# Two-layer mixed network on one core: the wave stage written out over two buffers, and five layers' loads issued ahead of their norms

## The chip, the core and the metric

The kernel runs on one core of a Trainium2 chip. A core has TensorE (matrix products), VectorE, ScalarE, GpSimd and a queue engine, SyncE, that issues transfers. They run side by side and meet at semaphores. The metric is the device time of one execution in microseconds (us).

## What is computed

`x` is 4 x 512 x 256 in float32. Six layers follow each other, each of the form x = x + f(norm(x)): a gated delta net, masked cross attention over 1601 context rows, a ternary MLP, a selective scan followed by a wave term, full cross attention over the same context, and a mixture of 8 experts. The wave term is what the change is mostly about. It takes the scan layer's own intermediate sum `xa`, normalises it, and does this for each of the 4 sequences:

```
v  = ln(xa) * g + b
uu = v @ W_si + b_si                       # 512 x 256, columns in 16 heads
up = pad(uu, 2 rows at either end, edge)
ux   = (up[3:-1] - up[1:-3]) * 0.5
uxx  = up[3:-1] - 2 uu + up[1:-3]
uxxx = (up[4:] - 2 up[3:-1] + 2 up[1:-3] - up[:-4]) * 0.5
du   = gate0 * sin(uu) + gate1 * (-6 uu ux - uxxx) + gate2 * (1 + alpha uu) * uxx
x    = x + xa + (0.1 * du) @ W_so + b_so
```

## The kernel before

`x` stays in on-chip memory as 128 partitions x 16 tiles x 256 (`c.x`), where a tile is 128 tokens and a sequence ("batch", b) is 4 tiles. `layernorm` writes a normalised and transposed copy to `c.xnT`: VectorE takes statistics of 16 tiles (L135, L138), ScalarE the root (L154), VectorE normalises (L147) in four groups of four tiles, TensorE transposes (L171), ScalarE copies out (L158). With `keep` the normalised rows are also kept in plain order.

Work is staged in `Scope`s. Each opens a `Block` with one program per engine; where the block closes, all engines meet at a barrier, and a scope that owns semaphores also clears them and meets once more (L46 to L50). `Chain.link` makes an engine wait for its own last instruction.

In the masked attention, the MLP, the scan and the full attention, `layernorm` comes first and then a scope whose main block has a SyncE program that loads the weights. Other engines of that block wait for those loads: in the masked attention GpSimd first widens the mask (L1389), then spreads a bias (L1403), on which TensorE's first product hangs; in the MLP TensorE waits for the first weight (L2232); in the scan GpSimd adds `b_out` to `xa` (L2423), and VectorE's first instruction (L2538) waits for that; in the full attention GpSimd copies a bias (L1847). The scan layer first loads its norm parameters in a block of their own (L2318), and then runs two norms: the first one's transposed output is overwritten by the second one's. The experts layer is the exception: its loads stand in a block ahead of its norm.

The wave stage (`waves`) loops over the four batches. Per batch: TensorE makes u (L2741), ScalarE adds the bias and writes `up` with its edges (L2761, L2766), GpSimd makes d1, f, kdv and d2 (L2784 to L2789), VectorE reduces the angle (L2804 to L2810), ScalarE takes the sine (L2770), VectorE makes the heat term (L2812 to L2817), combines all into `du` (L2820 to L2829), TensorE multiplies by W_so (L2748) and VectorE adds four tiles to x (L2837). Every tile has one buffer. Ahead of the loop GpSimd adds b_so to xa and xa to x (L2775, L2777), and VectorE's loop waits for both.

## Time and profile before

| | |
|---|---|
| median of 3 runs | 5632.72 us (5630.48 to 5633.34) |
| the profiled execution's own time | 5629.68 us |
| its span in the profile | 5627.8 us |
| mean granted TensorE clock | 0.95 of full speed |

The span runs from the first to the last instruction that the profiler saw. A timeline row gives: start (us from the span's start), duration (us), engine, line, operation, output and inputs, shapes, count (xN: N instructions merged into the row), and in brackets how long the engine was idle before it and what ended that. PE is TensorE, DVE VectorE, ACT ScalarE, POOL GpSimd; SPq and PEq are the sequencers of SyncE and TensorE, and a wait that ends with "PEq L50" or "L46" ended at a barrier. Digits are left out of tile names, so `ss_ln` stands for the scan layer's three norms and `wave_d` for d1 and d2. A windows row gives a stretch, its length, the busy us and instructions of TensorE, its weight loads, VectorE, ScalarE and GpSimd, the granted TensorE clock (1.00 is 2.4 GHz, 0.50 is 1.2 GHz), the share of the DMA engines and GB/s.

### The profile page before, as it was taken

The numbers are of one execution on the slowest core, as the hardware profiler recorded it, in microseconds if no ns is written. First come the engines' busy times: TensorE is split into PE (matmuls) and PEld (weight loads), VectorE is DVE, ScalarE is ACT, GpSimd is POOL, SyncE is SP. The second block draws the span as 40 slices with busy tenths as digits, with TensorE's granted clock in tenths as the row PEclk, the third lists the DMA queues.
The fourth block names the chain that finished last, engine by engine and source line by source line (L and its number), as shares of the span: only waits on it lengthen the run. The fifth ranks groups of instructions, "written<-read, shape, count | busy, mean of one in ns | idle before, by whom it ended". The sixth has DMA issues, their size and how long they took to land. (4 is left out here: it accounts for less than half of the span.)

```text
span 5627.8 us, 89667 instructions
## 1 busy us (share of the span) xinstructions
PE 4899.7 (87%) x37226; PEld 2802.5 (50%) x37226; DVE 2999.9 (53%) x5862; ACT 2219.3 (39%) x3543; POOL 1062.9 (19%) x660
## 2 busy tenths in 40 slices
PE   6879995999999999999899985666636999999897
PEld 3468884666666666666444442222213333333465
DVE  5757773555555555555100016778855666666360
ACT  5733432444444444444111114555512544445421
POOL 0145552111011011000000004446631000000021
PEclk9989997999999999999999997899867999999898
DMA  2221111000000000000200000000001000000122
GB/s 86 113 80 48 48 45 41 9 7 27 7 9 23 10 10 18 9 7 4 84 0 0 0 0 28 0 0 0 0 5 38 1 13 1 13 1 1 55 79 104
DMA packets 45384, 144.11 MB, mean 26 GB/s; under 512 B 6928, under 2 KB 18768, under 8 KB 38240
## 3 DMA queue, kind: packets, MB, share of 16 engines
q1 hardware_dynamic: 43472, 134.55, 6.7%
q8 instruction: 278, 4.55, 0.3%
q0 software_dynamic: 1536, 4.20, 0.2%
q14 instruction: 98, 0.80, 0.0%
HBM read 102.69 MB, written 36.04 MB: 25 GB/s over the span
## 5 line engine op out<-in xcount | busy, mean ns | idle before, releaser
L1471 DVE CUSTOM_DVE_ANT_0 ma_prob<-ma_ring,ma_mask 128x400 f32<-128x400 f32 (+1 forms) x1024 | 527.4, 572 | 260.0 <-PE ma_ring L1575 260.0
L1915 DVE TENSOR_REDUCE fa_part<-fa_ring 128x1 f32<-128x512 f32 x768 | 487.1, 681 | 221.9 <-PE fa_ring L2036 202.6
L1862 ACT ACTIVATE fa_prob<-fa_ring 128x512 f32<-128x512 f32 (+1 forms) x832 | 441.6, 598 | 407.6 <-PE fa_ring L2036 329.3
L2036 PE MATMUL fa_ring<-fa_K,fa_Q 32*128 32x512 f32 (+1 forms) x2048 | 532.2, 547 | 2.0
L1484 DVE COPY ma_PT<-ma_ring 128x512 f32<-128x512 f32 x512 | 342.0, 689 | 287.3 <-PE ma_ring L1585 286.9
L1585 PE MATMUL ma_ring<-ident,ma_prob 128*128 128x128 f32 (+1 forms) x3328 | 462.2, 280 | 6.7 <-ACT ma_prob L1430 6.7
L2056 PE MATMUL fa_ring<-fa_Qm,fa_K 32*128 32x512 f32 (+1 forms) x1664 | 458.8, 631 | 2.3 <-DVE fa_Qm L1932 2.3
L1599 PE MATMUL ma_pv<-ma_PT,ma_V 128*64 128x256 f32 (+1 forms) x3328 | 457.8, 393 | 0.0
L2245 PE MATMUL ffn_mid<-ffn_hid,ffn_h 128*128 128x512 f32 x1024 | 441.5, 593 | 9.7 <-DVE ffn_hid L2211 6.3
L1397 POOL TENSOR_SCALAR ma_diag<-ident,ma_rtotal 128x128 f32<-128x128 f32 x256 | 149.7, 602 | 1533.1 <-DVE ma_rtotal L1489 1533.1
L1585 PEld LDWEIGHTS ma_ring<-ident,ma_prob 128*128 128x128 f32 (+1 forms) x3328 | 357.1, 141 | 163.6 <-issue 105.1
L1575 PE MATMUL ma_ring<-ma_K,ma_Q 64*128 64x400 f32 (+1 forms) x2048 | 415.1, 523 | 0.0
L1430 ACT ACTIVATE ma_prob<-ma_prob,ma_neg 128x1601 f32<-128x1601 f32 x256 | 414.6, 1620 | 0.0
L1436 ACT ACTIVATE ma_PT<-ma_ring 128x512 f32<-128x512 f32 (+1 forms) x320 | 189.9, 593 | 481.7 <-PE ma_ring L1585 481.7
L2433 POOL TENSOR_TENSOR scan_dBx<-scan_dtx,scan_Bs 128x2048 f32<-128x2048 f32 x64 | 289.4, 4525 | 280.5 <-DVE scan_dtx L2577 217.6
L1599 PEld LDWEIGHTS ma_pv<-ma_PT,ma_V 128*64 128x64 f32 (+1 forms) x3328 | 198.9, 136 | 264.3 <-issue 178.7
L2245 PEld LDWEIGHTS ffn_mid<-ffn_hid,ffn_h 128*128 128x128 f32 x1024 | 193.9, 190 | 257.3 <-issue 247.8
L2588 DVE TENSOR_TENSOR_SCAN scan_h<-scan_dA,scan_dBx 128x512 f32<-128x512 f32 x256 | 292.8, 1205 | 39.2 <-POOL scan_dBx L2433 21.0
L2641 PE MATMUL scan_y<-scan_hC,ident 128*128 128x512 f32 x544 | 264.3, 631 | 11.1 <-DVE scan_hC L2594 11.1
L2217 DVE TENSOR_TENSOR ffn_scaled<-ffn_low,ffn_w_s 128x256 f32<-128x256 f32 x16 | 6.8, 425 | 493.1 <-PE ffn_low L2254 493.1
L2056 PEld LDWEIGHTS fa_ring<-fa_Qm,fa_K 32*128 32x128 f32 (+1 forms) x1664 | 140.2, 179 | 239.2 <-ACT fa_prob L1862 158.1
L1575 PEld LDWEIGHTS ma_ring<-ma_K,ma_Q 64*128 64x128 f32 x2048 | 176.9, 186 | 150.0 <-issue 69.4
(381 smaller groups left out, 7853.8 us busy)
## 6 DMA issues: line engine op xcount, KB each, us to landing
gd_rows<-gp_tile SPq DMA_DIRECT2D x16, 1024.0 KB, 4.2
gd_c_vg<-gd_rows SPq DMA_DIRECT2D x16, 1024.0 KB
moe_w<-in_moe_w SPq DMA_DIRECT2D x16, 1024.0 KB, 7.1
ma_w<-in_ma_w SPq DMA_DIRECT2D x32, 384.0 KB, 3.1
gd_rows<-gp_gate SPq DMA_DIRECT2D x16, 512.0 KB, 5.1
gd_c_qk<-gd_rows SPq DMA_DIRECT2D x16, 512.0 KB
ffn_h<-in_ffn_h SPq DMA_DIRECT2D x2, 4096.0 KB, 22.7
ma_ctxT<-in_ctxT SPq DMA_DIRECT2D x4, 1601.0 KB, 6.6
```

What stands on the lines that cost most here:

```text
L1430: nc.scalar.activation(rows, rows, ACT.Exp, bias=neg[:, t, h:h + 1], scale=SCALE, accum_out=total[:, t, h:h + 1]).then_inc(exp_ready, 1)
L1471: nc.vector.tensor_tensor_reduce(prob[:, u % 2, t, h, k0:k0 + width], bank("S", u, t, n, h)[:, 0:width], mask[:, b % 2, half * 2 + t, k0:k ...
L1484: nc.vector.tensor_copy(PT[0:n, (u * KT + kt) % NPT, :, :], bank("T", u, kt)[0:n, :].rearrange("p (h q) -> p h q", h=2)).then_inc(dve_take ...
L1575: nc.tensor.matmul(bank("S", u, t, n, h)[:, 0:width], Q[rows, q % 2, q0:q0 + P], K[rows, q % 2, k0:k0 + width], start=True, stop=True).the ...
L1585: last = nc.tensor.transpose(bank("T", u, kt)[0:n, h * QH + t * P:h * QH + (t + 1) * P], prob[:, u % 2, t, h, kt * P:kt * P + n], c.ident[:])
L1599: last = nc.tensor.matmul(pv[u % 2][cols, 0:QH], V[0:n, q % 2, kt, cols], PT[0:n, (u * KT + kt) % NPT, h, :], start=(kt == 0), stop=(kt == ...
L1862: nc.scalar.activation(prob[0:n, (u * KT + kt) % PROBS, j, :], bank("scores", u, kt, j)[0:n, :], ACT.Exp, scale=SCALE).then_inc(p_ready, 1)
L1915: ins = nc.vector.tensor_reduce(part[:, u % 2, t, j, n:n + 1], src[:], AX, ALU.max)
L2036: last = nc.tensor.matmul(bank("chunk", u, i)[:, at * w:(at + 1) * w], Q[rows, b % 2, g, tile * P:(tile + 1) * P], K[rows, b % 2, g, k0:k0 ...
L2056: nc.tensor.matmul(bank("scores", u, kt, j)[0:n, :], K[rows, b % 2, g, kt * P:kt * P + n], Qm[rows, u % 2, :], start=True, stop=True).then ...
L2245: last = nc.tensor.matmul(mid[m % 2][:], w[n][:, k, m * P:(m + 1) * P], hid[e][:, k, :], start=(k == 0), stop=(k == MH - 1))
L2588: nc.vector.tensor_tensor_scan(h[:, m, :], dA[m % 2][:], dBx[:, k, m, :], 0.0, ALU.mult, ALU.add).then_inc(scanned, 1)
```

## The change

Three things are done.

1. In the masked attention, the MLP, the scan and the full attention the first loads move from the main block's SyncE program into a load block that stands ahead of `layernorm`, as the experts layer has it. In the masked attention these are 7 loads, in the MLP 10, in the scan 13 with the norm parameters, in the full attention 9. The scan layer's block for the norm parameters alone is gone.
2. `layernorm` with `dst=None` leaves out ScalarE's copies and TensorE's transposes (the loop over groups in both). The scan layer's first norm is called so.
3. `waves` is rewritten. Its 6 loads and GpSimd's two sums (now x + xa and then + b_so, both into x) stand in a load block ahead of the norm. `up`, angle, sine, d1, d2, f, kdv, heat, du and the PSUM tiles of u and out have two buffers, by b % 2. The loops are written out: VectorE runs `shape(b + 1)` (the angle and the heat term) before `combine(b)` (the terms into du), and `add_out(b - 1)` after it; the output is added in two instructions of two tiles instead of four of one.

```diff
 def layernorm(...):
-            for g in range(GROUPS):
+            for g in range(GROUPS if dst is not None else 0):
...
 def masked_attention(...):
-    layernorm(nc, c, "ma_ln", c.x, c.xnT)
...
+        with Scope(nc, "ma_load") as first:
+            block = first.block()
+            @block.sync
+            def _(sp):
+                sp.dma_start(w[:, 0], c.dram["ma_w"][0]).then_inc(w_loaded[0], 16)
+                for dst, src in ((bias, "b"), (wo, "wo")):
+                    sp.dma_start(dst[:], c.dram[f"ma_{src}"]).then_inc(loaded, 16)
+                sp.dma_start(bo[:], c.dram["ma_bo"].partition_broadcast(P)).then_inc(loaded, 16)
+                sp.dma_start(ctxT[:], c.dram["ctxT"][0]).then_inc(ctx_loaded, 16)
+                sp.dma_start(mask8[:], c.dram["ma_mask"][0].rearrange("t p s -> p t s")).then_inc(mask_loaded, 16)
+                sp.dma_start(w[:, 1], c.dram["ma_w"][1]).then_inc(w_loaded[1], 16)
+        layernorm(nc, c, "ma_ln", c.x, c.xnT)
...
 def scan_channels(...):
+        with Scope(nc, "scan_load") as first:
...
+                sp.dma_start(ln[:], c.dram["scan_ln"]).then_inc(norms_loaded, 16)
+                for dst, src in ((win, "win"), (b_in, "bin"), (convw, "conv"), (conv_b, "conv_b"), (wxp, "wxp"), (wdt, "wdt"),
+                                 (b_dt, "bdt"), (neg_a, "A_log"), (skip, "skip"), (wout, "wout"), (pick, "pick")):
+                    sp.dma_start(dst[:], c.dram[f"scan_{src}"]).then_inc(loaded, 16)
+                sp.dma_start(b_out[:], c.dram["scan_bout"].partition_broadcast(P)).then_inc(loaded, 16)
+                sp.wait_ge(norms_loaded, 16)
+        layernorm(nc, c, "ss_ln0", c.x, None, keep=xa)
+        layernorm(nc, c, "ss_ln1", xa, c.xnT, gain=ln[:, 0, :], shift=ln[:, 1, :])
...
 def waves(...):
+        with Scope(nc, "wave_load") as first:
...
+            @block.gpsimd
+            def _(pool):
+                nc.gpsimd.tensor_tensor(c.x[:], c.x[:], xa[:], ALU.add).then_inc(based, 1)
+                pool.wait_ge(based, 1)
+                pool.wait_ge(loaded, LOADS)
+                nc.gpsimd.tensor_tensor(c.x[:], c.x[:], b_so[:].unsqueeze(1).broadcast_to([P, NT, D]), ALU.add).then_inc(based, 1)
+        layernorm(nc, c, "ss_ln2", xa, c.xnT, gain=ln[:, 2, :], shift=ln[:, 3, :])
...
         def _(pe):
+            inward(0)
+            inward(1)
+            for b in range(B):
+                if b + 2 < B:
+                    inward(b + 2)
+                outward(b)
...
         def _(act):
+            def take(b):
                 act.wait_ge(u_ready, b + 1)
+                if b >= 2:
+                    act.wait_ge(du_ready, b - 1)
+                    act.wait_ge(kdv_ready, b - 1)
...
+            take(0)
+            take(1)
+            for b in range(B):
+                take_sine(b)
+                if b + 2 < B:
+                    take(b + 2)
...
         def _(dve):
+            def add_out(b):
+                dve.wait_ge(based, 2)
+                for h in range(2):
+                    rows = c.x[:, TB * b + 2 * h:TB * b + 2 * h + 2, :]
+                    dve.wait_ge(out_ready, 2 * b + h + 1)
+                    nc.vector.tensor_tensor(rows, rows, out_ps[b % 2][h][:], ALU.add).then_inc(added, 1)
+            shape(0)
+            for b in range(B):
+                if b + 1 < B:
+                    shape(b + 1)
+                combine(b)
+                if b >= 1:
+                    add_out(b - 1)
+            add_out(B - 1)
```

## Rows read from the trace of the kernel before

**Rows 1.** The page: the span, and busy time of each engine.

```profile
span 5627.8 us, 89667 instructions
...
PE 4899.7 (87%) x37226; PEld 2802.5 (50%) x37226; DVE 2999.9 (53%) x5862; ACT 2219.3 (39%) x3543; POOL 1062.9 (19%) x660
```

**Rows 2.** Timeline, from the wave stage's norm to its first batch.

```profile
4100.09 5.32 DVE L135 BATCH_NORM_STATS2 ss_ln_stats<-ss_xa 128x6 f32<-128x256 f32 x16 [1.43 <-PEq L50]
...
4117.74 0.33 SPq L2727 DMA_DIRECT2D wave_wsi<-in_wave_wsi  x1
...
4123.39 5.83 PE L2741 MATMUL wave_u<-xnT,wave_wsi 128*128 x8 [8.29 <-DMA wave_bso<-in_wave_bso]
...
4141.23 2.00 DVE L2804 TENSOR_SCALAR wave_turns<-wave_up 128x1024 f32<-128x1024 f32 x1 [17.97 <-POOL x L2777]
```

**Rows 3.** Timeline, the wave stage's third batch.

```profile
4204.03 1.28 ACT L2761 ACT_TABLE_LOAD   x1 [18.67 <-PE wave_u L2741]
...
4207.17 0.69 DVE L2804 TENSOR_SCALAR wave_turns<-wave_up 128x1024 f32<-128x1024 f32 x1 [5.13 <-ACT wave_up L2766]
...
4207.90 2.27 DVE L2805 TENSOR_SCALAR wave_turns<-wave_turns 128x1024 f32<-128x1024 f32 x1
...
4220.94 1.23 DVE L2817 TENSOR_TENSOR wave_heat<-wave_heat,wave_s 128x1024 f32<-128x1024 f32 x1
...
4227.64 6.61 PE L2748 MATMUL wave_out<-wave_wso,wave_du 128*128 128x256 f32 x16 [23.74 <-DVE wave_du L2829]
...
4234.41 1.41 DVE L2837 TENSOR_TENSOR x<-x,wave_out 128x256 f32 x4 [6.83 <-PE wave_out L2748]
```

**Rows 4.** Windows: the border into the wave stage, and its third batch.

```profile
4117.00:4121.00 4.00, 0.00 (x0) 0.00 (x0) 0.00 (x0) 0.05 (x1) 0.00 (x0) 0.56 0.33 78
4207.17:4240.96 33.79, 10.05 (x24) 6.54 (x24) 21.23 (x22) 5.19 (x8) 9.69 (x4) 0.60 0.00 0
```

**Rows 5.** Timeline, start of the experts layer.

```profile
5285.02 0.33 SPq L2899 DMA_DIRECT2D moe_router<-in_moe_router  x1
...
5289.89 0.64 SPq L2904 DMA_DIRECT2D moe_xs<-moe_zeros  x1
...
5291.21 5.33 DVE L135 BATCH_NORM_STATS2 moe_ln_stats<-x 128x6 f32<-128x256 f32 x16 [6.96 <-PEq L46]
```

**Rows 6.** Timeline, start of the masked attention.

```profile
875.47 5.32 DVE L135 BATCH_NORM_STATS2 ma_ln_stats<-x 128x6 f32<-128x256 f32 x16 [1.40 <-PEq L50]
...
892.15 0.34 SPq L1367 DMA_DIRECT2D ma_bias<-in_ma_b  x1
...
906.66 17.27 POOL L1389 TENSOR_SCALAR ma_mask<-ma_mask 128x1604 bf16<-128x1604 uint8 x4 [51.82 <-DMA ma_mask<-in_ma_mask]
```

**Rows 7.** Timeline, start of the ternary MLP.

```profile
2703.47 5.32 DVE L135 BATCH_NORM_STATS2 ffn_ln_stats<-x 128x6 f32<-128x256 f32 x16 [1.12 <-PEq L50]
...
2720.50 0.80 SPq L2184 DMA_DIRECT2D ffn_w_s<-in_ffn_w_s  x2
...
2732.21 3.39 PE L2232 MATMUL ffn_lin<-xnT,ffn_w 128*128 x4 [13.51 <-DMA ffn_w<-in_ffn_w]
```

**Rows 8.** Timeline, start of the scan layer.

```profile
3359.07 5.32 DVE L135 BATCH_NORM_STATS2 ss_ln_stats<-x 128x6 f32<-128x256 f32 x16 [3.38 <-PEq L50]
...
3376.01 5.33 DVE L135 BATCH_NORM_STATS2 ss_ln_stats<-ss_xa 128x6 f32<-128x256 f32 x16 [4.50 <-PEq L50]
...
3409.88 8.83 POOL L2423 TENSOR_TENSOR ss_xa<-ss_xa,scan_bout 128x4096 f32<-128x4096 f32 x1 [734.63 <-DMA scan_bout<-in_scan_bout]
```

**Rows 9.** Timeline, start of the full attention.

```profile
4268.91 5.33 DVE L135 BATCH_NORM_STATS2 fa_ln_stats<-x 128x6 f32<-128x256 f32 x16 [0.82 <-PEq L50]
...
4285.60 0.33 SPq L1835 DMA_DIRECT2D fa_wq<-in_fa_wq  x1
...
4294.51 0.61 POOL L1847 COPY fa_bv_wide<-fa_bv 128x512 f32<-128x512 f32 x1 [7.60 <-DMA fa_bo<-in_fa_bo]
```

More of the change, by code:

```diff
@@ L164, in _ @@
         def _(pe):
-            for g in range(GROUPS):
+            for g in range(GROUPS if dst is not None else 0):
                 pe.wait_ge(xn_ready, g + 1)
@@ L1714, in full_attention, with _ @@
         ctxT = s.sb("ctxT", [P, DC, S2])
+        loaded = s.sem("loaded")
+        ctx_loaded = s.sem("ctx_loaded")
+        with Scope(nc, "fa_load") as first:
+            block = first.block()
+            @block.sync
+            def _(sp):
+                for dst, src in ((wq, "wq"), (wk, "wk"), (bqk, "bqk"), (wv, "wv"), (wo, "wo"), (sums, "sums"), (bv, "bv")):
+                    sp.dma_start(dst[:], c.dram[f"fa_{src}"]).then_inc(loaded, 16)
+                sp.dma_start(bo[:], c.dram["fa_bo"].partition_broadcast(P)).then_inc(loaded, 16)
+                sp.dma_start(ctxT[:], c.dram["ctxT"][0]).then_inc(ctx_loaded, 16)
+        layernorm(nc, c, "fa_ln", c.x, c.xnT)
+        bv_wide = s.sb("bv_wide", [P, FG, P])
         K = s.sb("K", [P, 2, FG, S2])
@@ L2684, in _, with waves @@
                 sequence_end(pe, b)
-def waves(nc, c, xa):
+def waves(nc, c, xa, ln):
     EDGE = 2
@@ L2772, in _ @@
         @block.gpsimd
         def _(pool):
[L2774 to L2790 removed]
+            chain = Chain(pool, gps)
@@ L2796, in _, with shape @@
             dve.wait_ge(ready0, 1)
-            dve.wait_ge(based, 2)
-            with dve.Fori(0, B) as b:
-                chain = Chain(dve, vec, per=9 + DC)
-                chain.start(b)
+            def shape(b):
+                k = b % 2
                 dve.wait_ge(up_ready, b + 1)
-                dve.sem_inc(passed, 1)
-                chain.link(nc.vector.tensor_scalar(turns[:], at(2), 1 / (2 * np.pi), TO_WHOLE, ALU.mult, ALU.add))
+                chain.link(nc.vector.tensor_scalar(turns[:], at(b, 2), 1 / (2 * np.pi), TO_WHOLE, ALU.mult, ALU.add))
@@ L2816, in _, with combine @@
                 chain.link(last)
-                chain.link(nc.vector.tensor_tensor(heat[:], heat[:], s1[:], ALU.mult))
+                chain.link(nc.vector.tensor_tensor(heat[:, k], heat[:, k], s1[:], ALU.mult))
+            def combine(b):
+                k = b % 2
                 dve.wait_ge(kdv_ready, b + 1)
-                chain.link(nc.vector.scalar_tensor_tensor(out=kdv[:], in0=d2[:], scalar=-0.5, in1=kdv[:], op0=ALU.mult, op1=ALU.add))
-                dve.wait_ge(out_ready, b + START)
@@ L2823, in _ @@
-                dve.wait_ge(sine_ready, b + (1 + START))
-                dve.sem_inc(passed, 1)
+                chain.link(nc.vector.scalar_tensor_tensor(out=kdv[:, k], in0=d2[:, k], scalar=-0.5, in1=kdv[:, k],
+                                                          op0=ALU.mult, op1=ALU.add))
+                dve.wait_ge(sine_ready, b + 1)
                 for m in range(DC):
-                    chain.link(nc.vector.tensor_scalar(sine[:, m, :], sine[:, m, :], gates[:, 0, m:m + 1], None, ALU.mult))
@@ L2827, in _ @@
-                for k, term in ((1, kdv), (2, heat)):
+                    chain.link(nc.vector.tensor_scalar(sine[:, k, m, :], sine[:, k, m, :], gates[:, 0, m:m + 1], None, ALU.mult))
+                for g, term in ((1, kdv), (2, heat)):
                     for m in range(DC):
-                        last = nc.vector.scalar_tensor_tensor(out=du[:, m, :], in0=term[:, m, :], scalar=gates[:, k, m:m + 1],
-                                                              in1=(sine if k == 1 else du)[:, m, :], op0=ALU.mult, op1=ALU.add)
-                    if k == 1:
+                        last = nc.vector.scalar_tensor_tensor(out=du[:, k, m, :], in0=term[:, k, m, :], scalar=gates[:, g, m:m + 1],
+                                                              in1=(sine if g == 1 else du)[:, k, m, :], op0=ALU.mult, op1=ALU.add)
+                    if g == 1:
@@ L2832, in _ @@
                         chain.link(last)
                 last.then_inc(du_ready, 1)
-                for t in range(TB):
-                    row = c.x[:, ds(b * TB + t, 1), :].rearrange("p a d -> p (a d)")
-                    dve.wait_ge(out_ready, b + (1 + START))
-                    last = nc.vector.tensor_tensor(row, row, out_ps[t][:, 0:D], ALU.add)
-                last.then_inc(added, 1)
-                chain.close()
+            def add_out(b):
[4 more added lines that the diff above has]
+                    nc.vector.tensor_tensor(rows, rows, out_ps[b % 2][h][:], ALU.add).then_inc(added, 1)
@@ L2842 @@
+            shape(0)
+            for b in range(B):
+                if b + 1 < B:
[4 more added lines that the diff above has]
+            add_out(B - 1)
 NE = 8
```

194 lines of the change are left out of this document (81 added, 113 removed).

## The prediction

> **What bounds the kernel now.** I read the page first, for its busy shares. TensorE is busy for 4899.7 us of a span of 5627.8 us [rows 1], so most of the kernel is bound by matrix products that the change doesn't touch. What it touches are stretches in which TensorE stands still: five starts of a layer and the wave stage. I therefore read the timeline of each of those, engine by engine. A layer's chain crosses a barrier to the next one, so whatever time such a stretch loses comes off the span one for one.
>
> The wave stage shows three things. Its block opens at 4117.74, and VectorE's first real instruction starts only at 4141.23, after 17.97 us of waiting for GpSimd's sum into x [rows 2]. Then each batch is one serial chain: in the third, ScalarE starts at 4204.03, VectorE works from 4207.17, TensorE starts at 4227.64 and VectorE adds from 4234.41 [rows 3]. VectorE is busy for 21.23 us of a batch's 33.79, GpSimd for 9.69 [rows 4]. The stage ends where fa_ln begins, at 4268.91 less 0.82 of idleness, so at 4268.09 [rows 9]; it takes 150.35 us. At the other starts an engine waits for a load issued only after the norm [rows 6 to 9].
>
> **What a load block ahead of a norm costs.** The last layer already has one [rows 5]. VectorE's last instruction before it ends at 5291.21 - 6.96 = 5284.25, and the first load goes out at 5285.02 (0.77 later). Eleven loads end at 5290.53, so 0.50 us each, and the norm starts 0.68 later. So n loads delay a norm by 0.77 + 0.50 n + 0.68 less the gap that was there. The norm behind that block isn't slowed by its traffic: 16 statistics take 5.33 us, and 5.32 without it [rows 5, 6].
>
> **Masked attention** (7 loads): 4.95 - 1.40 = 3.55 us of delay; the block then opens at 892.15 + 3.55 = 895.70. GpSimd, which was held to 906.66 by the mask, starts at once [rows 6]. The loads needed at most 906.66 - 892.15 = 14.5 us, and are now issued from 874.84, so they have landed by 889.4. TensorE's first product hangs on GpSimd, so the gain is **11.0 us**.
>
> **Ternary MLP** (10 loads): 6.45 - 1.12 = 5.33 us; the block opens at 2725.83 and TensorE, whose first product waited for weights until 2732.21 [rows 7], starts there. Gain **6.4 us**. Its later, larger weights were ahead of their use and now leave some 17 us earlier: nothing.
>
> **Scan start** (13 loads, with the norm parameters first, whose own wait is inside the issuing): 7.95 - 3.38 = 4.57 us. The first norm loses its transposes and copies. VectorE's last instruction of it ended at 3376.01 - 4.50 = 3371.51 [rows 8]; it now ends at 3376.08, and with a gap of 0.82 as in [rows 9] the second norm starts at 3376.90. From a norm with gain to the next block are 4117.74 - 4100.09 = 17.65 us [rows 2], so that opens at 3394.55. GpSimd's sum, on which VectorE's first instruction waits, started at 3409.88 [rows 8] and now starts there. Gain **15.3 us**.
>
> **Full attention** (9 loads): 5.95 - 0.82 = 5.13 us; the block opens at 4290.73. GpSimd did 1.31 us of memsets (4285.60 to 4294.51 - 7.60) before its wait, so its copy starts at 4292.04 instead of 4294.51 [rows 9]. Gain **2.5 us**.
>
> **Wave start.** The two sums (x + xa, then + b_so) leave the main block, but they stand inside the load block, which closes before the norm opens. In every row that crosses such a border the next engine starts 0.7 to 1.4 us after the last work of the slowest one, so I take it that the norm waits for GpSimd: the sums run before the norm, not beside it. One sum of this size takes 8.83 us [rows 8]. They start at 4098.66 + 0.77 = 4099.43, end at 4117.15, and the norm starts at 4117.83 instead of 4100.09: 17.74 late. The six loads (3.0 us) hide behind them. The main block opens at 4135.48. TensorE's first product takes 5.83 us, as now, since the granted clock was 0.56 over the border, that is at its lower level for most of it [rows 2, 4]; then ScalarE takes 1.9 us from product to VectorE (4204.03 to 4207.17 less a table load of 1.28 [rows 3]). VectorE starts at 4143.3: **2.1 us later** than now. The gain must come from the batches.
>
> **Wave batches.** VectorE's program becomes shape(0), shape(1), combine(0), shape(2), combine(1), add(0), shape(3), combine(2), add(1), combine(3), add(2), add(3). In [rows 3] a shape lasts from 4207.17 to 4220.94 + 1.23 = 4222.17, 15.0 us, a combine from there to 4227.6, 5.4, the adds 1.4. Four shapes and combines are 81.6, the two adds ahead of the last du 2.8. Two stalls remain: shape(2) needs up(2), which ScalarE may write only after combine(0), and that is the instruction just ahead: 1.9 us; shape(3) likewise, but add(0) covers 1.4 of it: 0.5. Queued behind ScalarE's wait is sine(b+1), which VectorE needs only a shape later. Sum to the last du: 86.8 us. Then TensorE's products, 6.6 us [rows 3], hide add(2), and the last half add with its hop is 0.9: 94.3. The stage ends at 4143.3 + 94.3 = 4237.6 instead of 4268.1. Gain **30.5 us**.
>
> Bounds. *Table loads*: each batch now has two of 1.28 us, one of them on the chain [rows 3]. Written out, only the first sine should need one, off the chain; if each take needs one, 2.6 us come back. *The two engines together*: a VectorE instruction that takes 0.69 us beside an idle GpSimd port takes 2.26 beside a busy one (4207.17 and 4207.90 [rows 3]). My 15.0 holds that for a batch whose GpSimd work starts with it; batch 1's instead begins when batch 0's ends. Between no loss at all (some 6 us less) and the whole of GpSimd's 9.69 us lost (some 4 more) I keep 15.0, since the same instructions meet. *First product*: between half of 5.83 us, if the clock stayed at its upper level, which is twice the lower, and 5.83.
>
> The Trainium skill (SBUF — State Buffer, "Who interferes with whom") says that VectorE in a two-port mode or with two SBUF inputs and GpSimd exclude each other for whole instructions. The trace's 0.69 against 2.26 agrees; by that rule in full, shape(1) would last up to 19 us and the gain of the batches would be 26.5.
>
> One more semaphore lives to the end of the layer, so that ends with one more clearing and barrier: 0.3 us, the difference of the gaps 0.82 and 1.12 [rows 7, 9].
>
> **Sum.** 11.0 + 6.4 + 15.3 + 2.5 + 30.5 - 0.3 = 65.4 us. The profiled execution took 5629.68 us with its span of 5627.8; it comes to 5564.3. The median shown is 5632.72, 3.0 above, so my time is **5567 us**.
>
> **Rivals.** *The sums do run beside the norm* (chance 0.05). If the border doesn't hold the norm for GpSimd, it starts at 4098.66 + 0.77 + 3.0 + 0.68 = 4103.1, 14.7 earlier, less some contention in the norm: about 5554 us. Against it speaks that every engine's last instruction precedes every border that I read.
>
> *The wave pipeline gives little* (0.10): table loads on each take, full exclusion in shape(1), and code that runs once in place of a loop, for which no row has a price. With half of the 32.6 us that the batches give, the time is 5583. For it: VectorE alone already needs some 85 of the 127 us from 4141.2 to 4268.1. Against it: all work outside VectorE (sines, takes, products) has a shape or more to hide behind.
>
> *The loads pay nothing* (0.02): the waits that they replace end no earlier because what they gate was late anyway. Then only the delays remain, 3.6 + 5.3 + 0.8 + 5.1 = 14.8 us against 30 from the waves: 5617. Against it: the rows name the DMA as what ended each wait.
>
> *Slower* (0.02): transfers in flight slow the norms. Four norms of about 17 us have traffic beside them; to eat 65 us each would have to double. Row for row, the last layer's norm is unmoved (5.33 against 5.32), so this needs the new traffic to behave otherwise. It decides from 16 us per norm; at double that the time would be some 5698 us. The Trainium skill (SBUF — State Buffer, "SBUF: two separate sides") says that transfers and engines don't contend; the trace agrees.
>
> **How the numbers follow.** 0.81 for my forecast, with its own range of 5558 to 5576: first product 2.9 and shape(1) 6 us down, table loads and full exclusion 6.6 up, and two or three for the TensorE clock at each start. To hold 8 in 10 with margin for the sums beside the norm and for a weaker pipeline, the range is 5550 to 5583. A measurement of this kernel tells apart about 0.2%, 11 us. Faster by more: 0.97. Within: 0.01. Slower: 0.02.
>
> **What would show it.** The wave norm's first statistic some 17 to 19 us after the scan's last add, right behind GpSimd's second sum (right), or 3 to 5 after it (wrong). GpSimd's mask work, TensorE's first MLP product and GpSimd's scan sum within 1 us of their block's opening. In the wave stage one table load, VectorE waits of about 2 and 0.5 us ahead of shape(2) and shape(3), none ahead of shape(1) or a combine, and about 94 us from VectorE's first instruction to the stage's end. The prediction is wrong if a shape lasts over 17 us, if VectorE waits for sine or kdv, or if any layer outside these stretches changes its length by over 2 us.

## The result, and the profile after

The kernel after takes 5562.34 us (median of four executions: 5562.39, 5554.02, 5562.28, 5563.30), the kernel before 5633.03 us beside it (5630.48 to 5633.70). The ratio is 0.9872, with a 95% interval of 0.9855 to 0.9889. The change saves 70.7 us; forecast were 65.7 (5567 us).

The page of the kernel after answers to [rows 1]:

```profile
span 5560.5 us, 89468 instructions
...
PE 4891.6 (88%) x37194; PEld 2794.0 (50%) x37194; DVE 2998.5 (54%) x5854; ACT 2205.7 (40%) x3528; POOL 1063.4 (19%) x660
```

Each engine is busy for about as long as before. The time came out of idleness, so it has to be looked for at the borders of stages. I measure a stage from the end of VectorE's last instruction of one layer to that of the next (the start of a norm's first statistic less the idle time in its brackets).

| us | before | after | saved |
|---|---|---|---|
| gated delta net (untouched) | 874.08 | 875.07 | -1.0 |
| masked attention | 1828.28 | 1820.61 | 7.7 |
| ternary MLP | 653.34 | 647.34 | 6.0 |
| scan | 742.97 | 730.42 | 12.6 |
| wave term | 169.43 | 132.24 | 37.2 |
| full attention | 1016.16 | 1013.38 | 2.8 |
| experts (untouched) | 343.50 | 341.44 | 2.1 |

The two stages that no one touched moved by 1.0 and 2.1 us. Over all kernels of this study the first lay between 873.90 and 880.10 and the last between 341.30 and 344.48, so a single profile says nothing about a few us of a whole span; I compare stages.

The timeline of after at the four starts of a layer whose loads moved, against [rows 6 to 9]:

```profile
876.42 0.34 SPq L1265 DMA_DIRECT2D ma_w<-in_ma_w  x1
...
879.25 1.46 SPq L1271 DMA_DIRECT2D ma_w<-in_ma_w  x1
...
881.16 5.32 DVE L135 BATCH_NORM_STATS2 ma_ln_stats<-x 128x6 f32<-128x256 f32 x16 [6.09 <-PEq L46]
...
897.69 17.27 POOL L1398 TENSOR_SCALAR ma_mask<-ma_mask 128x1604 bf16<-128x1604 uint8 x4 [41.88 <-POOLq L50]
...
2702.33 5.33 DVE L135 BATCH_NORM_STATS2 ffn_ln_stats<-x 128x6 f32<-128x256 f32 x16 [6.65 <-PEq L46]
...
2719.50 3.43 PE L2254 MATMUL ffn_lin<-xnT,ffn_w 128*128 x4 [2.30 <-PEq L50]
...
3350.24 5.32 DVE L135 BATCH_NORM_STATS2 ss_ln_stats<-x 128x6 f32<-128x256 f32 x16 [7.22 <-PEq L46]
...
3381.14 8.83 POOL L2440 TENSOR_TENSOR ss_xa<-ss_xa,scan_bout 128x4096 f32<-128x4096 f32 x1 [712.55 <-SPq L46]
...
4211.43 5.33 DVE L135 BATCH_NORM_STATS2 fa_ln_stats<-x 128x6 f32<-128x256 f32 x16 [5.75 <-PEq L46]
...
4229.27 0.61 POOL L1864 COPY fa_bv_wide<-fa_bv 128x512 f32<-128x512 f32 x1
```

Two things stand in these rows. The norms start later after the layer before, 6.09 us where it was 1.40 in the masked attention, since seven issues now stand ahead of them. And none of them names a DMA as what ended a wait any more: the work behind the norm starts where the barrier opens.

The wave stage, against [rows 2, 3]:

```profile
4074.93 8.80 POOL L2734 TENSOR_TENSOR x<-x,ss_xa 128x4096 f32<-128x4096 f32 x1 [20.81 <-DVEq L46]
4083.81 8.80 POOL L2737 TENSOR_TENSOR x<-x,wave_bso 128x4096 f32<-128x4096 f32 x1
4092.96 5.32 DVE L135 BATCH_NORM_STATS2 ss_ln_stats<-ss_xa 128x6 f32<-128x256 f32 x16 [19.52 <-PEq L46]
...
4110.04 10.54 PE L2772 MATMUL wave_u<-xnT,wave_wsi 128*128 128x512 f32 x24 [2.22 <-PEq L50]
...
4113.81 1.27 ACT L2804 ACTIVATE wave_up<-wave_u,wave_bsi 128x512 f32<-128x512 f32 x2 [4.51 <-PE wave_u L2772]
...
4115.52 2.41 DVE L2848 TENSOR_SCALAR wave_turns<-wave_up 128x1024 f32<-128x1024 f32 x1 [5.31 <-ACT wave_up L2808]
...
4118.80 1.28 ACT L2816 ACT_TABLE_LOAD   x1
...
4124.38 2.87 POOL L2833 TENSOR_TENSOR wave_d<-wave_up 128x1024 f32<-128x1024 f32 x1
...
4135.51 1.23 DVE L2861 TENSOR_TENSOR wave_heat<-wave_heat,wave_s 128x1024 f32<-128x1024 f32 x1
4136.77 0.69 DVE L2848 TENSOR_SCALAR wave_turns<-wave_up 128x1024 f32<-128x1024 f32 x1
...
4144.66 1.23 DVE L2861 TENSOR_TENSOR wave_heat<-wave_heat,wave_s 128x1024 f32<-128x1024 f32 x1
...
4152.80 0.69 DVE L2848 TENSOR_SCALAR wave_turns<-wave_up 128x1024 f32<-128x1024 f32 x1 [1.71 <-ACT wave_up L2808]
...
4174.71 0.69 DVE L2848 TENSOR_SCALAR wave_turns<-wave_up 128x1024 f32<-128x1024 f32 x1 [0.52 <-ACT wave_up L2808]
...
4194.96 9.99 PE L2782 MATMUL wave_out<-wave_wso,wave_du 128*128 128x256 f32 x32 [16.48 <-DVE wave_du L2873]
...
4204.99 0.69 DVE L2884 TENSOR_TENSOR x<-x,wave_out 128x512 f32<-128x512 f32 x1 [0.97 <-PE wave_out L2782]
```

GpSimd's two sums run one behind the other in the load block, and the norm starts 0.35 us after the second has ended, 19.52 us after the scan's last add. Then VectorE works nearly without a gap: up to the last `du` its only waits are 1.71 us ahead of the third shape and 0.52 ahead of the fourth. The first shape ends at 4136.74 and takes 21.2 us, the second ends at 4145.89 and takes 9.1; the third and fourth take 15.0 each. GpSimd takes up the second batch at 4124.38, right behind the first, so that both batches' GpSimd work runs beside the first shape and none beside the second.

### The profile page after: what moved, and what is told of

It reads as the page before. It is cut to its first block and busy times, and to the rows that moved or that the text cites. A ratio compares the mean times of both kernels' runs of the same rounds, so it can differ in the third digit from the quotient of the medians.

```text
span 5560.5 us, 89468 instructions
## 1 busy us (share of the span) xinstructions
PE 4891.6 (88%) x37194; PEld 2794.0 (50%) x37194; DVE 2998.5 (54%) x5854; ACT 2205.7 (40%) x3528; POOL 1063.4 (19%) x660
```

## The experiments

All were timed beside the kernel before, whose median was 5633.59 us in the first group of runs, 5633.89 in the second and 5634.51 in the third. The stage lengths of each, as in the table above:

| us | masked att. | MLP | scan | waves | full att. | median |
|---|---|---|---|---|---|---|
| before | 1828.28 | 653.34 | 742.97 | 169.43 | 1016.16 | 5633.0 |
| after | 1820.61 | 647.34 | 730.42 | 132.24 | 1013.38 | 5562.3 |
| waves_only | 1828.75 | 654.74 | 741.37 | 132.33 | 1017.48 | 5596.0 |
| loads_only | 1818.45 | 645.77 | 727.26 | 170.10 | 1014.16 | 5598.4 |
| beside_whole | 1817.97 | 645.84 | 726.47 | 129.62 | 1013.87 | 5558.9 |
| beside_pieces | 1817.95 | 645.85 | 727.64 | 128.76 | 1013.40 | 5551.7 |
| unshifted | 1820.23 | 647.58 | 727.22 | 132.44 | 1013.31 | 5562.7 |
| pe_sums | 1820.28 | 647.55 | 727.37 | 119.68 | 1013.33 | 5552.5 |
| mask_beside | 1811.32 | 645.82 | 726.44 | 132.45 | 1014.43 | 5554.5 |
| all_three | 1808.05 | 645.69 | 727.51 | 118.23 | 1013.88 | 5537.8 |
| pe_sums2 | 1821.24 | 645.78 | 726.79 | 122.99 | 1013.46 | 5551.0 |
| pe_sums_unshifted | 1817.62 | 645.83 | 726.89 | 119.91 | 1013.32 | 5545.6 |
| all_three2 | 1809.74 | 647.76 | 727.21 | 118.26 | 1013.93 | 5537.3 |

### The two halves of the change: waves_only and loads_only

The first keeps the new `waves` and puts the four layers' loads back; the second does the reverse.

```diff
 waves_only: before.py, and in it
-        layernorm(nc, c, "ss_ln2", xa, c.xnT, gain=ln[:, 2, :], shift=ln[:, 3, :])
-        waves(nc, c, xa)
+        waves(nc, c, xa, ln)                 # with the whole new waves()
 loads_only: after.py, and in it
-        waves(nc, c, xa, ln)
+        layernorm(nc, c, "ss_ln2", xa, c.xnT, gain=ln[:, 2, :], shift=ln[:, 3, :])
+        waves(nc, c, xa)                     # with the whole old waves()
```

> The kernel before with the new wave stage alone (double buffers, order, sums in a load block ahead of its norm). My theory, that the stages' gains are independent of each other and the wave stage gives 37.2 us of the 67.3 (169.43 to 132.24 us from the scan's last add to the stage's last add): 5633 - 37 = 5596 us, and the wave stage lasts 132 us. Rival, that part of that gain is a by-product of the earlier starts (another TensorE clock): under 31 us, 5602 or more.

> The changed kernel with the old wave stage and its norm: loads ahead of four norms and the first scan norm without transposes. Theory: the four starts give 9.97 (masked attention, to GpSimd's mask work), 6.0 (MLP), 12.6 (scan) and 2.8 us (full attention), of which some 2 are lost again inside the attention: 5633 - 29 = 5604 us, and together with waves_only the gains add up to 66 to 70. Rival, that only the wave part matters: 5625 or more.

Measured: 5595.97 us (5595.22 to 5596.54), ratio 0.9933 [0.9916, 0.9950], and 5598.39 us (5594.29 to 5600.83), ratio 0.9937 [0.9920, 0.9953]. The waves save 37.6 us, the loads 35.2, together 72.8 against 70.7 for both: the halves add up within what can be measured. The table says the same by stage: each half moves its own rows, and the others by at most 1.6 us. waves_only came out as I had expected. loads_only is 6 us faster than the 5604 that I had taken from the stages of after: its masked attention, MLP and scan are 2.2, 1.6 and 3.2 us shorter than there, though their code is the same (where after lost time in the masked attention and in the scan is shown below).

For the wave stage I cut each kernel's length in three: from the scan's last add to VectorE's first real instruction of the stage (start), from there to the end of the last `du` (batches), and from there to the last add into x (tail).

| us | start | batches | tail | sum |
|---|---|---|---|---|
| after | 42.08 | 85.66 | 4.50 | 132.24 |
| waves_only | 42.15 | 85.68 | 4.50 | 132.33 |
| beside_whole | 39.45 | 85.67 | 4.50 | 129.62 |
| beside_pieces | 38.59 | 85.68 | 4.50 | 128.77 |
| unshifted | 42.10 | 83.50 | 6.83 | 132.43 |
| pe_sums | 27.37 | 85.70 | 6.62 | 119.69 |
| pe_sums2 | 29.49 | 85.68 | 7.82 | 122.99 |
| pe_sums_unshifted | 29.52 | 83.50 | 6.90 | 119.92 |
| all_three2 | 27.40 | 83.51 | 7.35 | 118.26 |

The batches repeat to 0.04 us within one order of the work. Start and tail move with the place of the sums and the order, and by some 2 us with the clock that TensorE was granted for its first and its last products.

### Sums beside the norm: beside_whole and beside_pieces

In the change the sums stand before the norm, and hold it. Here GpSimd's program is handed into `layernorm`'s own block, once as two instructions of 16 tiles, once as 8 + 8 instructions of two tiles.

```diff
-def layernorm(..., keep=None):
+def layernorm(..., keep=None, beside=None):
+        if beside is not None:
+            block.gpsimd(beside)
...
+        STEP = 16                            # beside_pieces: 2
+        def sums(pool):                      # was: GpSimd's program in the load block
+            for t in range(0, NT, STEP):
+                rows = c.x[:, t:t + STEP, :]
+                nc.gpsimd.tensor_tensor(rows, rows, xa[:, t:t + STEP, :], ALU.add).then_inc(based, 1)
...
+        layernorm(nc, c, "ss_ln2", xa, ..., beside=sums)
```

> The changed kernel, but GpSimd's two sums stand inside the norm's own block, so that they do run beside the norm. The norm then starts some 4.4 us after the scan's last add instead of 19.5, 15.1 earlier. If GpSimd and VectorE don't hinder each other the time is 5562 - 15 = 5547. If they exclude each other for whole instructions, VectorE's 16 normalising instructions (which start 7.2 us into the norm) wait for a sum of 8.8 us, perhaps for both: the norm lasts 2 to 10 us longer, 5549 to 5557. Rival, that the border doesn't hold the norm in the changed kernel either: 5562.

> As beside_whole, but each sum in eight pieces of two tiles (some 1.1 us each) in place of one. If the engines exclude each other for whole instructions, VectorE waits for one piece at a time and both end together: GpSimd's remaining 10.5 us and VectorE's 5.4 us of normalising take turns, so the norm is 6 to 10 us longer: 5553 to 5557. If the exclusion lets VectorE in between pieces at little cost it is better than beside_whole by up to 8 us: 5549.

Measured: 5558.91 us (5554.39 to 5560.39), ratio 0.9865 [0.9848, 0.9881], and 5551.73 us (5551.60 to 5554.14), ratio 0.9856 [0.9839, 0.9872]. Timeline of beside_whole over the norm:

```profile
4074.02 8.82 POOL L2740 TENSOR_TENSOR x<-x,ss_xa 128x4096 f32<-128x4096 f32 x1 [22.36 <-SPq L46]
...
4081.22 12.58 DVE L150 TENSOR_SCALAR ss_ln_xn<-ss_xa,ss_ln_mv,ss_ln_rstd 128x256 f32<-128x256 f32 x8
...
4082.91 8.80 POOL L2745 TENSOR_TENSOR x<-x,wave_bso 128x4096 f32<-128x4096 f32 x1
```

The same x8 row taken apart, its first scaling and its second:

```profile
4081.22 1.77 DVE L150 TENSOR_SCALAR ss_ln_xn<-ss_xa,ss_ln_mv,ss_ln_rstd 128x256 f32<-128x256 f32 x1
...
4082.91 8.96 DVE L150 TENSOR_SCALAR ss_ln_xn<-ss_xa,ss_ln_mv,ss_ln_rstd 128x256 f32<-128x256 f32 x1
```

And of beside_pieces:

```profile
4077.87 14.99 DVE L150 TENSOR_SCALAR ss_ln_xn<-ss_xa,ss_ln_mv,ss_ln_rstd 128x256 f32<-128x256 f32 x16
...
4080.59 10.18 POOL L2745 TENSOR_TENSOR x<-x,wave_bso 128x512 f32<-128x512 f32 x8
```

Eight of the norm's scalings take 2.67 us where GpSimd is idle (the same rows of pe_sums2). In beside_whole they took 12.58: they began at 4081.22 and ended at 4093.80, 2.1 us behind the end of GpSimd's second sum (4091.71). The first scaling was held through the tail of one GpSimd instruction (to 4082.84) and then had its turn; the second was held through the whole of the next one and took 8.96 us; the other six took 0.40 each. So the engines take turns, one instruction of each, and what a turn costs VectorE is the length of GpSimd's instruction. In pieces they take turns too: ten scalings take 1.35 to 1.52 us each beside pieces of 1.3, the last six 0.40, and all sixteen are done in 14.99 us. The statistics ahead of the scalings aren't held: sixteen take 5.3 us beside the first sum as without it.

The start of the stage came only 2.6 and 3.5 us earlier, out of the 14.9 by which the norm's first statistic came earlier (4.61 us after the scan's last add, against 19.52). In beside_whole 9.9 us of the rest went into the two held scalings, and 1.7 us into TensorE's first product, at its lower clock here: VectorE waited 7.01 and 6.96 us for `up` after the block opened, 5.31 in after. So "beside the norm" is nearly as long as "before the norm".

The two do overlap: from the first sum to TensorE's first product are 35.1 us in after (4074.93 to 4110.04) and 27.7 in beside_whole (4074.02 to 4101.68), 7.5 less, about the 7.2 us of the norm that lie ahead of its first scaling. But in after the sums start 1.5 us behind the scan's last add and hide the block's six issues, while in beside_whole norm and sums both start 4.6 us behind it. That takes 3.1 of the 7.5 back, and the lower clock the 1.7.

The difference of 7 us between the two medians isn't in the wave stage, where they differ by 0.9 us; in their profiles most of it is the untouched first and last stage, so it says nothing on the sums. By the stages the theory of exclusion for whole instructions held, the norm even somewhat longer than the 2 to 10 us that I had given it, and pieces in place of whole sums brought 0.9 us, not up to 8.

The Trainium skill (SBUF — State Buffer, "Who interferes with whom") calls the port pair of VectorE and GpSimd an exclusive lock. The rows agree: the scaling at 4082.91 takes 8.96 us beside a sum of 8.80.

### The order without the shift: unshifted

```diff
-            shape(0)
             for b in range(B):
-                if b + 1 < B:
-                    shape(b + 1)
+                shape(b)
                 combine(b)
```

> The changed kernel, but VectorE's order in the wave stage is shape(b), combine(b), add_out(b - 1): double buffers without the shift by a batch. My theory: the shift gives nothing, since sine(b) and kdv(b) are ready before shape(b) ends, and costs the two waits for ScalarE's take (1.71 and 0.52 us in the changed kernel's trace). The wave stage's 132.24 us become 130, the time 5560. Rival, that the shift is what hides sine and kdv: VectorE waits ahead of every combine, 1 us or more each, 5563 to 5568.

Measured: 5562.71 us (5554.11 to 5563.78), ratio 0.9869 [0.9852, 0.9885]. The stage takes 132.4 us either way, but by other parts. The batches take 83.50 us, 2.16 less: the waits of 1.71 and 0.52 us are gone. The tail takes 2.33 more. I had expected a stage of 130 us and had priced the waits alone; the rival, a wait ahead of each combine, isn't there either. Timeline of unshifted at its end:

```profile
4197.19 1.42 DVE L2873 SCALAR_TENSOR_TENSOR wave_du<-wave_heat,wave_gates,wave_du 128x512 f32<-128x512 f32 x2
...
4198.66 6.05 PE L2782 MATMUL wave_out<-wave_wso,wave_du 128*128 128x256 f32 x16 [10.18 <-DVE wave_du L2873]
```

The last 16 products take 6.05 us after 10.18 us in which TensorE stood still. In after, both last groups of 16 run back to back in 9.99 us (the row at 4194.96), so the second one is done 3.8 us after its `du` at 4201.18. The windows of after show the clock, ahead of these products and over them:

```profile
4186.00:4194.90 8.90, 0.00 (x0) 0.00 (x0) 8.65 (x13) 0.35 (x1) 0.00 (x0) 0.50 0.00 0
4194.90:4205.70 10.80, 9.99 (x32) 7.85 (x32) 8.70 (x14) 0.00 (x0) 0.00 (x0) 0.74 0.00 0
```

It was granted at its lower level (0.50) while the engine idled, and came up within the 32 products: over the last 16 of them (4201.20 to 4204.95) it is 1.00, over the 16 of unshifted 0.50 in the first 3 us and 0.71 in the rest. So what the shifted order brings on this path is not the hiding of ScalarE's and GpSimd's work, since the unshifted one waits less. It brings the last but one product next to the last.

### The sums in TensorE: pe_sums, pe_sums2, pe_sums_unshifted

GpSimd's two sums are dropped, and TensorE adds xa and b_so in PSUM by products with the identity.

```diff
-            @block.gpsimd                    # both sums gone
...
             def outward(b):
-                pe.wait_ge(du_ready, b + 1)
                 if b >= 2:
                     pe.wait_ge(added, 2 * (b - 1))
+                for h in range(2):           # pe_sums: for each tile alone
+                    t0 = TB * b + 2 * h
+                    nc.tensor.matmul(out_ps[b % 2][h][:], c.ident[:], xa[:, t0:t0 + 2, :], start=True, ...)
+                    nc.tensor.matmul(out_ps[b % 2][h][:], c.ident[:], <b_so over both tiles>, start=False, ...)
+                pe.wait_ge(du_ready, b + 1)
...                                            # the products of du with start=False
```

> The changed kernel without GpSimd's two sums of the wave stage: TensorE adds xa and b_so into the output's PSUM tile by products with the identity, issued before it waits for du. Theory, that the sums delayed the norm by their whole length because the border waits for GpSimd: the norm starts 4.4 us after the scan's last add in place of 19.5, undisturbed, and the time is 5562 - 15 = 5547. Rival, that the added products (8 per batch, 256 columns each) end up on the chain of the last batch: 5550.

> Only the two sums are taken from GpSimd and given to TensorE; the order of the wave batches stays shifted. For each pair of tiles of a batch TensorE multiplies the identity by the two tiles of xa (512 columns) and by the bias laid out over both tiles (512 columns), and the products of du are added on top in the same PSUM bank. Nothing is left out of the computation. In the profile of the changed kernel the border of the load block came 17.9 us late because it waited for GpSimd's two sums. Theory (the border is the whole price of the sums): the wave stage becomes about 132.2 - 17.9 = 114.3 us, plus what the identity products cost on the path: the earlier form of this placement had 119.7 us, since the last batch's identity products stood behind the products before them and were some 2.3 us late. Four long products for each batch in place of eight short ones have the same columns, so I expect 119 to 120 us again and a median of 5551 (5547 to 5555), 11 us below the changed kernel. Rival 1 (the sums beside other work cost something of their own, as contention): then the gain stays under 8 us, 5555 or more. Rival 2 (long products are cheaper, since each of the short ones had a start of its own): stage 117 to 118, 5549.

> As the run before, with the order of VectorE's parts put back to shape(b), combine(b), add_out(b-1). Theory (shifting the order hides the waits of 1.7 and 0.5 us but TensorE then idles before the last products and runs them at a lower clock, which takes the gain back): the order makes no difference that can be measured, the stage is 118 to 120 us and the median within 3 us of the run before. Rival (the identity products stand in front of the last products of du only while the order is shifted, since they wait for the adds of two batches earlier, which the unshifted order does sooner): then the stage is about 2.3 us shorter than the run before, 117 us.

pe_sums, and all_three below, have a product with `start=True` for each of the two tiles that share a PSUM tile, and leave out a part of xa and b_so: by the order of the products that of the first of each two tiles, which I argue and no run shows tile by tile. pe_sums2 and the others have one such product over both tiles and leave out nothing.

Measured: 5552.48 us (5548.55 to 5553.70), ratio 0.9853 [0.9837, 0.9870]; 5551.00 us (5549.14 to 5556.25), ratio 0.9856 [0.9841, 0.9871]; 5545.63 us (5543.22 to 5547.06), ratio 0.9842 [0.9827, 0.9857]. Timeline of pe_sums2 at the end of the stage:

```profile
4178.73 6.42 PE L2778 MATMUL wave_out<-wave_wso,wave_du 128*128 128x256 f32 x16 [13.04 <-DVE wave_du L2869]
4184.99 1.02 PE L2773 MATMUL wave_out<-ss_xa,ident 128*128 128x512 f32 x2
...
4188.42 3.62 PE L2778 MATMUL wave_out<-wave_wso,wave_du 128*128 128x256 f32 x16
```

And of pe_sums_unshifted:

```profile
4175.81 1.02 PE L2774 MATMUL wave_out<-wave_bso,ident 128*128 128x512 f32 x2
...
4183.51 6.12 PE L2778 MATMUL wave_out<-wave_wso,wave_du 128*128 128x256 f32 x16 [6.68 <-DVE wave_du L2869]
```

The norm again starts 4.61 us after the scan, and now nothing stands beside it: the start shrinks by 14.7 us where the first product found a fast clock (pe_sums), by 12.6 where it didn't (pe_sums2). That is the price of the sums in the change. Not all is kept. In the shifted order the last `du` is ready at 4184.95, but TensorE must first do the identity products, and begins at 4188.42, 3.5 us late; the tail is 3.3 us longer than in after. Without the shift they are done 6.7 us before the last `du`, so the last products start at once, though at the lower clock again (6.12 us): batches and tail together take 90.40 us against 93.50. That is the rival of pe_sums_unshifted, and it gives 3.1 us where I had named 2.3; my theory, by which the order makes no difference, fell. The 119 to 120 us that I expected of pe_sums2 were too low (122.99): its start is 2.1 us longer than that of pe_sums, 1.7 of it the first product, and its last but one group of products took 6.42 us against 5.21, so that the identity products behind them came later. Against the change the three kernels save 9.3 to 12.6 us of the stage, not the 14.9 by which the norm came earlier. For pe_sums I had expected 5547 us, or 5550 with the identity products on the last batch's chain; they are on it.

### GpSimd's mask work beside the norm: mask_beside

The mask's load goes out first, and GpSimd's first widening of it runs in the norm's block of the masked attention.

```diff
 ma_load:
+                sp.dma_start(mask8[:], ...)   # now the first of the seven
                 sp.dma_start(w[:, 0], ...)
...
+        def widen_first(pool):
+            pool.wait_ge(mask_loaded, 16)
+            for t in range(TB):               # the four instructions of widen_mask(0, t)
+                nc.gpsimd.tensor_scalar(mask[:, 0, t, :], ...).then_inc(mask_ready, 1)
+        layernorm(nc, c, "ma_ln", c.x, c.xnT, beside=widen_first)
```

> The changed kernel, with the mask's load issued first and GpSimd's widening of the first mask (4 instructions of 4.32 us) in the block of masked attention's norm. Without exclusion 17.3 us would go off the chain, 5545. By exclusion for whole instructions as in beside_whole, GpSimd has the first 7.2 us of the norm for itself and then VectorE's normalising waits for one to three of its instructions: GpSimd's next work starts 6 to 10 us earlier than in the changed kernel, 5552 to 5556.

Measured: 5554.48 us (5546.11 to 5556.90), ratio 0.9856 [0.9839, 0.9872]; the stage takes 1811.32 us against 1820.61. Timeline of mask_beside:

```profile
885.25 17.27 POOL L1282 TENSOR_SCALAR ma_mask<-ma_mask 128x1604 bf16<-128x1604 uint8 x4 [25.89 <-DMA ma_mask<-in_ma_mask]
...
891.97 12.31 DVE L150 TENSOR_SCALAR ma_ln_xn<-x,ma_ln_mv,ma_ln_rstd 128x256 f32<-128x256 f32 x8
...
912.30 5.38 PE L1641 MATMUL ma_ring<-ma_wo,ma_wide 128*128 128x256 f32 x16 [3.01 <-POOL ma_wide L1419]
```

The widening keeps its 17.27 us and pushes the norm's scalings to 12.31 again, but norm and mask overlap: TensorE's first product comes 33.60 us after the stage's beginning (878.70) instead of 41.14. The other 1.8 us of the 9.3 come later in the stage, where after loses 2.3 us in one clock dip (below) that this profile doesn't have. Here "beside" pays: in after the norm (16.5 us from 881.16 to 897.69) and the mask (17.3) stood one behind the other, 33.9 us; now they take 26.3 together (884.78 to about 911.1, where GpSimd's next instruction starts). The overlap is the same 7.5 us as with the sums, and the lengths are alike too (17.3 us of GpSimd work here, 17.6 there). What differs is what is lost beside it: here the mask stood behind the issues in both kernels, so nothing is taken back.

### All together: all_three and all_three2

The edits of mask_beside, of unshifted, and of pe_sums (all_three) or pe_sums2 (all_three2).

> unshifted, pe_sums and mask_beside together. If they are independent, 2 + 15 + 8 = 25 us below the changed kernel: 5537. Rival, that GpSimd and VectorE or the TensorE clock take part of it back: 5542 or more.

> Unshifted order, the sums in TensorE, and the mask's load first with GpSimd's first widening of it beside the norm of the masked attention. Nothing is left out of the computation. Theory (the three places are apart in time, so their gains add): 5562.3 - 11 (sums) - 8 to 9 (mask) + 0 (order) = 5543; by stages, waves 118 to 120 us, masked attention 1808 to 1811 us. The earlier form of this combination had a median of 5537.8 (5530.4 to 5540.4), so 5536 to 5545. Rival (the gain of the head start in masked attention is lost again where TensorE's clock dips): masked attention 1811 or more, median 5545 or more.

Measured: 5537.77 us (5530.35 to 5540.42), ratio 0.9830 [0.9814, 0.9847], and 5537.28 us (5532.97 to 5538.33), ratio 0.9827 [0.9813, 0.9840]. all_three2, which leaves out nothing, is 25 us faster than the change. By stages: 14.0 us in the waves, 10.9 in the masked attention. Both lie where I had expected them (5537, and 5536 to 5545), and the gains of the places add up.

## Why the prediction was right, and where its sum was lucky

The time lay 4.7 us below the forecast of 5567, inside the narrow range. Stage by stage the touched ones gave 66.2 us, where 65.4 were forecast (65.7 by the rows below, and -0.3 for one more clearing, which can't be seen apart). But that agreement is partly one of errors that cancel.

| term, us | forecast | measured where the work starts | measured over the stage |
|---|---|---|---|
| masked attention | 11.0 | 9.97 | 7.7 |
| MLP | 6.4 | 6.04 | 6.0 |
| scan | 15.3 | 16.07 | 12.6 |
| full attention | 2.5 | 2.83 | 2.8 |
| wave start | -2.1 | 0.5 | |
| wave batches with tail | 32.6 | 36.7 | 37.2 (with the start) |

**The head starts were right.** From the row of the experts layer came 0.77 + 0.50 n + 0.68 us for a norm behind n loads. It gives 4.95, 6.45, 7.95 and 5.95 us; the brackets of the four norms are 6.09, 6.65, 7.22 and 5.75. The first is 1.1 us over: one issue took 1.46 us (the row at 879.25) where most take 0.4 to 0.5, and the first issue went out 1.35 us behind VectorE's last instruction in place of 0.77. That is the missing us of the masked attention.

**What was not in the sum: the clock behind a head start.** In the masked attention the lead of 10.0 us was kept until some 1335 us into the stage; there 2.3 us went. In the scan about 3 us went right at the start: VectorE's first scan instruction stands 46.10 us behind its first convolution (3390.51 to 3436.61), in loads_only and unshifted 43.12. The windows of after show the place in the masked attention:

```profile
2205.00:2210.00 5.00, 2.80 (x21) 1.49 (x18) 3.37 (x11) 0.60 (x1) 0.37 (x1) 1.00 0.81 336
2210.07:2215.07 5.00, 5.00 (x14) 1.70 (x15) 0.66 (x3) 0.69 (x1) 0.00 (x0) 0.66 0.02 5
2215.07:2220.00 4.93, 4.93 (x36) 2.84 (x37) 4.44 (x17) 2.21 (x3) 0.00 (x0) 1.00 0.00 0
```

The timeline of after, one row of the scan's start:

```profile
3402.42 6.71 PE L2640 MATMUL scan_B<-scan_xc,scan_wxp 128*112 128x512 f32 x8 [2.95 <-ACT scan_xc L2485]
```

and the same products in loads_only:

```profile
3399.40 5.13 PE L2641 MATMUL scan_B<-scan_xc,scan_wxp 128*112 128x512 f32 x8 [2.94 <-ACT scan_xc L2486]
```

The clock fell to 0.66 in a stretch in which TensorE was busy all the time, and the same eight products take 5.13 or 6.71 us, which is 1.6 of the 3. loads_only has neither loss (1818.45 and 727.26 us), with the same code in these stages. So it is not a cost of the loads; it is where the clock happens to move. I had allowed "two or three for the TensorE clock at each start", which covers it.

**The wave start was right in its mechanism and 2.6 us off in size.** The border waits for GpSimd: the norm's first statistic came 19.52 us after the scan's last add, 18.1 later than before, where 17.7 were forecast, and the rival in which the sums run beside the norm fell. The term that was mis-sized is the first product, 5.83 us: it took 3.8 us until ScalarE started at 4113.81, 0.9 more than the lower bound that I had named, and 2.1 of the 2.6. I had taken the product's clock from the border of before, where TensorE stands still for 8.29 us until a DMA lands [rows 2] and the clock is 0.56 [rows 4]. The change takes that wait away. TensorE now stands still for 2.22 us behind the norm's last transpose, and the clock of the norm is still granted. The windows of after show it, over the border and over the first 4 us of this product:

```profile
4107.90:4109.90 2.00, 0.00 (x0) 0.00 (x0) 0.00 (x0) 1.40 (x3) 0.00 (x0) 1.00 0.00 0
4110.00:4114.00 4.00, 3.96 (x10) 1.84 (x11) 0.17 (x1) 0.18 (x1) 0.00 (x0) 1.00 0.00 0
```

and in pe_sums2:

```profile
4092.00:4096.00 4.00, 3.88 (x5) 1.71 (x6) 0.17 (x1) 0.00 (x0) 0.00 (x0) 0.57 0.00 0
```

Ten products against five in the same time. In beside_whole, beside_pieces, pe_sums2 and pe_sums_unshifted the same product met the lower clock behind 2.2 to 2.6 us of standing still, in the others the upper one behind 2.2 to 2.3, so neither value holds for the code alone.

**The wave batches.** To the last `du` 86.8 us were forecast and 85.66 came, with the waits of 1.9 and 0.5 us as 1.71 and 0.52, and one table load off the chain. But the shapes agree with the forecast only in their sum: 21.2 + 9.1 + 15.0 + 15.0 = 60.3 us, where four times 15.0 were forecast. I had written that GpSimd's work for batch 1 begins when batch 0's ends, and still priced it beside shape(1). It was done at 4134.80, beside shape(0). A shape takes 9.1 us without GpSimd's work beside it, and each batch's work adds about 6 (15.0 with one, 21.2 with two), so for the sum it doesn't matter which shape meets it. I hadn't worked that out, so that the sum came right was luck. The sign that I had set myself, a shape of over 17 us, has come true, and it says rightly that this part of the picture was wrong. The 1.1 us come from the combines (5.2 us each, not 5.4) and the adds. The tail was forecast at 7.5 us (6.6 for cold products and 0.9) and took 4.50. The step that failed is the sentence that took the products' 6.6 us from the old batch: the written-out order puts two groups of products back to back, and I didn't read that off my own list of steps. Of the 6.7 us by which the stage beat the forecast, 2.6 are the start, 1.1 the batches and 3.0 the tail.

**The rivals.** Sums beside the norm: not so in this change, and when made so, worth 2.6 to 3.5 us of the stage, not nearly the 14.7 from which I had taken off only "some contention in the norm": in beside_whole the contention alone is 9.9. A weak pipeline: no. Loads that pay nothing: no. Transfers that slow the norms: no, a norm's statistics take 5.32 or 5.33 us behind every load block.

**Outside the change** the last layer moved by 2.1 us, over the 2 that I had named as a sign of error. In other kernels the untouched first and last stage move by as much and more, so the bound was too tight.

What stays open: one of four executions of after, one of unshifted and one of mask_beside took some 8 us less than the others (5554.02 against 5562.3). No profile was taken of such an execution. One profile is of an execution well below the others of its kernel, that of all_three (5530.35 us, the others 5536 to 5540): against all_three2 its span is 7.3 us shorter, 3.8 in the first layer, 1.7 in the masked attention and 2.1 in the MLP. That points to many small clock dips rather than one, but doesn't settle it. Why one kernel's first wave product or scan products meet the upper clock and another's the lower, with the same code there, stays open as well.

## What to carry to other kernels

Loads in a block ahead of a norm cost half a us of issue each and pay whatever the next block waited for; read both numbers from rows, the gain is the smaller of the old wait and the whole norm, less the issues. Work that has no deadline (a residual, a bias) costs its full length if it stands in a block whose border others wait for. Put beside a norm on GpSimd, 17 to 18 us of it overlapped by 7.5 us in both places tried here, since the norm's scalings were held and its statistics were not; count against that what the work had hidden where it stood before. Given to an engine that is idle there, it took 9.3 to 12.6 us off the stage. Before writing out an order by hand, list the tail: here the clock of the last products went by what ran right before them, and work queued ahead of it in the same engine counts fully.

## What the runs showed of the hardware that I had not expected

- VectorE's scalings and GpSimd take turns by single instructions, even where GpSimd's stand only 0.07 us apart: beside two sums of 8.8 us one scaling ran between them and the next took 8.96 us, beside pieces of 1.3 us ten scalings took 1.35 to 1.52 each, beside the mask's 4.25 two took 4.41 each. Short pieces bring VectorE more turns but hardly an earlier end (0.9 us here). The norm's sixteen statistics take 5.3 us with or without GpSimd's work.
- TensorE's clock is not a function of the code at a place alone. In the table of starts, batches and tails VectorE waits 5.31 us for the first `up` in five kernels and 6.96 to 7.01 in four, and the same eight scan products take 5.12 to 5.38 or 6.71 us.
- The 10.18 us in which TensorE stood still before the last products cost about 2.3 us (6.05 against 3.8), which is as much as all waits that the shifted order had.
- Now and then an issue on SyncE takes over a us instead of 0.4 to 0.5, and not always the same one: in the masked attention's block the last of seven took 1.46 in after, the third 1.39 in mask_beside, the last 2.16 in pe_sums2.
